# Linear attention: the inverses of the diagonal blocks are doubled from 16 to 64 rows in small array squares, and the solve substitutes between the two halves of 64 rows

## What is computed

```python
def _step(S, xs):
    qt, kt, vt, gt, bt = xs
    S = S * jnp.exp(gt)[..., None, None]
    pred = jnp.einsum('bhk,bhkv->bhv', kt, S)
    delta = (vt - pred) * bt[..., None]
    S = S + jnp.einsum('bhk,bhv->bhkv', kt, delta)
    return (S, jnp.einsum('bhk,bhkv->bhv', qt, S))
...
q = l2norm(q) * dk ** (-0.5)
k = l2norm(k)
...
o = o * jax.lax.rsqrt(jnp.mean(o * o, -1, keepdims=True) + EPS) * norm_weight
o = o * jax.nn.silu(gate)
return o.reshape(b, t, VALUE_DIM) @ Wo
```

## Time and profile before

| | us |
|---|---|
| median of 3 runs | 1380.96 |
| lowest, highest | 1378.22, 1382.22 |
| the profiled execution, its own time | 1384.09 |
| its span | 1382.5 |

### The profile page before, as it was taken

One profiled execution on the slowest core, in us unless ns is written; L12 is line 12 of the kernel. 1 busy time (PEld: TensorE's weight loads), 2 busy tenths in 40 slices (PEclk: granted clock), 3 DMA queues, 4 the chain that ended last, 5 costly groups with the idle time before them and its releaser, 6 DMA issues. The chain is left out here.

```text
span 1382.5 us, 24134 instructions
## 1 busy us (share of the span) xinstructions
PE 1207.8 (87%) x8826; PEld 1027.0 (74%) x8826; DVE 881.8 (64%) x2593; ACT 612.7 (44%) x1559; POOL 94.7 (7%) x103
## 2 busy tenths in 40 slices
PE   4999999899999974999899997279999999898478
PEld 3888789788878873888788897257777777677255
DVE  3767376375737656666567565688778887775423
ACT  3635454353444433434343432455675557444211
POOL 1000000000000001000000001110222022211000
PEclk9999999999999976999999996669999999999689
DMA  8010000000000020000000001100000000000322
GB/s 277 1 62 1 1 1 1 0 0 0 0 1 1 1 85 0 1 1 0 3 1 0 1 1 48 53 9 20 27 27 2 27 28 27 2 2 2 99 71 98
DMA packets 25722, 33.96 MB, mean 25 GB/s; under 512 B 4781, under 2 KB 21005, under 8 KB 25613
## 3 DMA queue, kind: packets, MB, share of 16 engines
q1 hardware_dynamic: 25612, 32.52, 7.2%
HBM read 30.34 MB, written 2.17 MB: 24 GB/s over the span
## 5 line engine op out<-in xcount | busy, mean ns | idle before, releaser
L986 PE MATMUL b_ps<-ln_high,b_high 128*128 128x512 f32 x256 | 102.2, 399 | 26.1 <-PEq L61 20.9
L333 DVE TENSOR_REDUCE a_negmax<-a_ps 128x1 f32<-128x128 f32 x128 | 37.2, 291 | 115.5 <-PE a_ps L514 106.9
L986 PE MATMUL b_ps<-ln_high,b_low 128*128 128x512 f32 x256 | 101.9, 398 | 0.0
L986 PE MATMUL b_ps<-ln_low,b_high 128*128 128x512 f32 x256 | 101.8, 398 | 0.0
L889 DVE TENSOR_TENSOR gate_up_raw<-gate_up_raw,b_ps 128x512 f32<-128x512 f32 x64 | 43.2, 686 | 91.7 <-PE b_ps L986 59.6
L553 PE MATMUL a_ps<-a_wo_high,a_oT 128*128 128x256 f32 x512 | 94.9, 284 | 2.0 <-DVE a_oT L359 2.0
L1013 PE MATMUL b_ps<-b_wd_high,b_mid 128*128 128x256 f32 x512 | 96.4, 283 | 0.0
L945 ACT ACTIVATE gate_up_raw<-b_ps 128x512 f32<-128x512 f32 x64 | 37.5, 598 | 121.0 <-PE b_ps L986 120.9
L477 PE MATMUL a_ps<-ln_high,a_w_high 128*128 128x512 f32 x160 | 69.1, 432 | 15.5 <-PEq L61 15.5
L553 PEld LDWEIGHTS a_ps<-a_wo_high,a_oT 128*128 128x128 f32 x512 | 79.7, 189 | 2.9 <-DVE a_oT L359 2.9
L1013 PEld LDWEIGHTS b_ps<-b_wd_high,b_mid 128*128 128x128 f32 x512 | 80.7, 189 | 0.6
(11 more groups left out here) (356 smaller groups left out, 3118.1 us busy)
## 6 DMA issues: line engine op xcount, KB each, us to landing
d_slots<-in_D_packed SPq DMA_DIRECT2D x16, 433.0 KB, 4.7
c_a_all<-a_scratch SPq DMA_DIRECT2D x8, 768.0 KB, 3.7
x<-in_hidden SPq DMA_DIRECT2D x4, 512.0 KB, 10.6
...
```

What stands on the lines that cost most here:

```text
L986: mm = nc.tensor.matmul(ps[:, bank, :], wpart, xpart, start=(j == 0), stop=(j == len(passes) - 1))
```

## The change

The block diagonal of 16x16 inverses isn't spread to 128x128 any more. VectorE's `seeds` writes the inverses into 32-wide rows (`inv16T`) and transposes them (`inv16`). TensorE then doubles them: `pair_part` and `pair_inverses` form the missing 16x16 corners of the 32x32 inverses, as products of 32x32x32 on single squares of the array (48 and 84 products for the 12 units); `quarter_part` and `quarter_inverses` form the corners of the upper and lower 64x64 inverses (24 and 36 such products). VectorE's `join_pairs` subtracts; ScalarE copies the results out and places them into `firstT` and `secondT` (`place_second`, `place_first`, `place_off`: nine instructions on 32 partitions). `half_part` forms, for each unit, the block under the diagonal times the lower inverse (12 products of 64x64x64). `solve` applies the two 64x64 inverses to the right side with a stationary operand of 128x64, `substitute` subtracts from the lower 64 rows what the solved upper rows give (12 products, 64x64 stationary). The four `step`s, N, its transpose and its square, `copy_n`, `copy_z` and POOL's `inverses` are gone. `copy_y` is done by row halves, four times.

The orders of TensorE, VectorE and ScalarE are changed too: `scores(m, 0)` goes ahead of jobs 0 and 1, `turn_values` goes up, jobs 4 and 5 go behind `outputs(s, 0)`, `project_out` and `all_norms` go down; on ScalarE `solved_keys` stays behind `silu(c, 2)`; on VectorE `keep_state`, `second_values` and `mean_square` go up among the columns, and `join_pairs` stands between `products` 3 and convolutions 3 to 5. PSUM banks are dealt anew, and `turn_out(d)` waits for the values of d+2. The core of the diff (indentation cut; first VectorE, then ScalarE, then TensorE):

```diff
+    def seeds(m):
+        nc.vector.tensor_tensor(
+            inv16T[:].rearrange("p u (b t) -> p u b t", b=2),
+            inv[:, :, 1:SUB + 1].rearrange("p u (o t) -> p u o t", o=1).to_broadcast([P, UNITS, 2, SUB]),
+            sides[:].rearrange("p (o b k) -> p o b k", o=1, k=1).to_broadcast([P, UNITS, 2, SUB]),
+            ALU.mult).then_inc(S["seed_ready"], 1)
+        dve.wait_ge(S["seed_ready"], at("seed_ready", m, 1))
+        nc.vector.transpose(flat(inv16[:]), flat(inv16T[:])).then_inc(S["seed_ready"], 1)
+
+    def join_pairs(b):
+
+        dve.wait_ge(S["a_done"], at("a_done", b, 1))
+        if b >= 1:
+            dve.wait_ge(S["half_copied"], at("half_copied", b - 1, 2))
+        nc.vector.tensor_tensor(flat(inv32T[:]), flat(inv16T[:]), ps[:, INV32_BANKS[0], 0:WIDE32],
+                                ALU.subtract).then_inc(S["pair_ready"], 1)
+        dve.wait_ge(S["a_done"], at("a_done", b, 2))
+        nc.vector.tensor_tensor(flat(inv32[0:96]), flat(inv16[0:96]), ps[0:96, INV32_BANKS[1], 0:WIDE32],
+                                ALU.subtract).then_inc(S["pair_ready"], 1)
...
         run(m, column_sum, 1)
         for h in range(DH):
             run(c, scan, h)
-        run(c, convolve, 6, 7)
-        run(m, columns, 2, 3)
-        run(c, convolve, 7, 8)
-        run(m, columns, 3, 4)
-        run(c, convolve, 8, 9)
-        run(s, step, 1, 0)
+        run(c, convolve, 6, 9)
+        run(m, columns, 2, 4)
+        run(s, keep_state)
+        run(m, off_diagonal, 0)
         run(m, columns, 4, 5)
-        run(s, step, 1, 1)
-        run(m, off_diagonal, 0)
-        run(m, columns, 5, 6)
         run(m, off_diagonal, 1)
-        run(m, columns, 6, 7)
-        run(s, step, 2, 0)
-        run(m, column_product, 7)
-        run(s, step, 2, 1)
+        run(m, columns, 5, 7)
         run(m, off_diagonal, 2)
-        run(m, column_sum, 7)
-        run(m, column_product, 8)
+        run(m, columns, 7, 8)
+        run(s, second_values)
         run(c, convolve, 9, 10)
-        run(m, column_sum, 8)
+        run(m, columns, 8, 9)
         run(c, convolve, 10, 11)
-        run(m, column_product, 9)
-        run(s, step, 3, 0)
-        run(m, column_sum, 9)
+        run(m, columns, 9, 10)
         run(c, convolve, 11, 12)
-        run(s, step, 3, 1)
+        run(s, mean_square, 0)
         run(m, column_product, 10)
         run(c, convolve, 12, 13)
         run(m, column_sum, 10)
-        run(s, keep_state)
+        run(c, convolve, 13, 14)
         run(m, column_product, 11)
-        run(c, convolve, 13, 14)
+        run(c, convolve, 14, 15)
         run(m, column_sum, 11)
-        run(c, convolve, 14, 15)
+        run(s, mean_square, 1)
         run(m, column_product, 12)
-        run(s, second_values)
+        run(c, convolve, 15, 16)
         run(m, column_sum, 12)
-        run(c, convolve, 15, 16)
+        run(d, add_out)
         run(m, column_product, 13)
-        run(s, mean_square, 0)
+        run(c, convolve, 16, 17)
         run(m, column_sum, 13)
-        run(c, convolve, 16, 17)
+        run(c, keys)
         run(m, column_product, 14)
-        run(d, add_out)
+        run(c, convolve, 17, 18)
         run(m, column_sum, 14)
-        run(c, keys)
-        run(m, column_product, 15)
-        run(c, convolve, 17, 18)
-        run(m, column_sum, 15)
-        run(s, mean_square, 1)
-        run(m, first_inverse)
+        run(m, columns, 15, 16)
+        run(m, seeds)
         if d == LAST:
...
                 channels.tap(act, c, j)
-        for q in range(PAIRS + 1):
-            run(s, copy_n, q)
+        run(s, copy_part16)
+        run(m, values_by_token, 0)
+        run(m, values_by_token, 1)
+        run(s, place_second)
+        run(s, copy_part32)
+        run(s, place_first)
         if d == LAST:
             n.copy(act, ps, 0)
         run(d, copy_oT, 0)
         if d == LAST:
             n.copy(act, ps, 1)
             n.copy(act, ps, 2)
-        run(s, copy_n, PAIRS + 1)
-        run(s, copy_n, PAIRS + 2)
+        run(s, place_off)
         run(m, fold_even)
         if inside(c):
             channels.silu(act, c, 0)
             channels.silu(act, c, 1)
-        for q in range(2 * PAIRS, 3 * PAIRS):
-            run(s, copy_n, q)
+            channels.tap(act, c, 2)
+            channels.tap(act, c, 3)
+        run(s, copy_part64)
         run(s, copy_y, 0)
         run(s, copy_y, 1)
-        if inside(c):
-            channels.tap(act, c, 2)
         run(m, second_keys)
-        run(s, copy_z, 0)
-        run(s, copy_z, 1)
-        run(m, values_by_token, 0)
-        run(m, values_by_token, 1)
-        if inside(c):
-            channels.tap(act, c, 3)
+        run(s, copy_y, 2)
+        run(s, copy_y, 3)
         if inside(c):
             channels.silu(act, c, 2)
+        run(s, solved_keys)
+        run(c, all_squares)
+        run(s, copy_wkT)
+        if inside(c):
             channels.tap(act, c, 4)
             channels.tap(act, c, 5)
-        run(c, all_squares)
-        run(s, solved_keys)
-        run(s, copy_wkT)
         run(s, squares, 0)
         run(s, save_output, 0)
...
+    def pair_part(b):
+
+        pe.wait_ge(S["seed_ready"], at("seed_ready", b, 1))
+        pe.wait_ge(S["l_ready"], at("l_ready", b, PAIRS))
+        if b + 1 < BATCH:
+            pe.wait_ge(S["conv_step"], at("conv_step", b + 1, CONVS))
+        for u in range(UNITS):
+            for q, rows in enumerate(QUARTERS):
+                mm = nc.tensor.matmul(ps[rows, PART16_BANK, cols32(u)], low[rows, b % 2, u, rows],
+                                      inv16T[rows, u, :], start=True, stop=True)
...
+    def half_part(b):
+
+        upper, lower = HALF_ROWS
+        if b == 0:
+            pe.wait_ge(S["cleared"], at("cleared", 0, 1))
+        pe.wait_ge(S["half_copied"], at("half_copied", b, 1))
+        for i, us in enumerate(UNIT_SETS):
+            for u in range(us.start, us.stop):
+                mm = nc.tensor.matmul(ps[upper, PART64_BANKS[i], cols64(u)], low[lower, b % 2, u, upper],
+                                      secondT[lower, u, :], start=True, stop=True)
...
+        src = right[:, b % 2, s]
+        for i, (h, half, cols) in enumerate(rights(s)):
+            for rows, inverse in zip(HALF_ROWS, (firstT, secondT)):
+                mm = nc.tensor.matmul(ps[rows, SET_BANKS[s], cols], inverse[:, h * HALVES + half, :],
+                                      src[:, cols], start=(i == 0), stop=False, skip_group_check=True)
...
+    def substitute(b, s):
+
+        upper, lower = HALF_ROWS
+        pe.wait_ge(S["pc_copied"], at("pc_copied", b, 2))
+        pe.wait_ge(S["y_copied"], at("y_copied", b, s + 1))
+        for h, half, cols in rights(s):
+            mm = nc.tensor.matmul(ps[lower, SET_BANKS[s], cols], part64[upper, h * HALVES + half, :],
+                                  y[upper, s, cols], start=False, stop=True, skip_group_check=True)
...
     for t in range(BATCH + 2):
         c, m, s, d = t + 1, t, t - 1, t - 2
+        run(m, scores, 0)
         run(c, job, 0)
         run(c, job, 1)
-        run(m, scores, 0)
-        run(s, n_product, 0)
-        run(s, n_product, 1)
-        run(s, n_product, 2)
+        run(s, pair_part)
         run(m, scores, 2)
-        run(s, n_product, 3)
+        run(m, turn_values, 0)
+        run(m, turn_values, 1)
+        run(s, pair_inverses)
         if d == LAST:
             pe.wait_ge(S["saved"], at("saved", LAST, 2))
             n.turn(pe, ps, r.ident, 0)
             n.turn(pe, ps, r.ident, 1)
+        run(s, quarter_part)
         run(d, turn_out, 0)
         run(d, turn_out, 1)
         if d == LAST:
             n.turn(pe, ps, r.ident, 2)
-        run(s, n_product, 4)
         run(m, scores, 4)
-        for q in range(PAIRS + 2, 3 * PAIRS):
-            run(s, n_product, q)
-        run(s, solve_blocks, 0)
-        run(s, solve_blocks, 1)
+        run(s, quarter_inverses)
+        run(s, half_part)
+        run(s, solve, 0)
+        run(s, solve, 1)
         run(c, job, 2)
         run(c, job, 3)
+        run(s, substitute, 0)
+        run(s, substitute, 1)
         run(m, turn_keys)
-        run(s, step, 0, 0)
-        run(s, step, 0, 1)
-        run(m, turn_values, 0)
-        run(m, turn_values, 1)
-        run(s, step, 1, 0)
-        run(s, step, 1, 1)
         run(m, turn_low, 0)
         run(m, turn_low, 1)
-        run(s, step, 2, 0)
-        run(s, step, 2, 1)
+        run(s, new_state)
         run(m, turn_low, 2)
-        run(c, job, 4)
-        run(s, step, 3, 0)
-        run(s, step, 3, 1)
-        run(c, job, 5)
-        run(s, new_state)
-        run(d, project_out, 0)
         run(s, turn_solved_keys)
         run(s, outputs, 0)
-        run(c, all_norms)
+        run(c, job, 4)
+        run(c, job, 5)
         run(s, known)
+        run(d, project_out, 0)
         run(d, project_out, 1)
         run(s, outputs, 1)
+        run(c, all_norms)
         run(m, gates, 0)
         run(m, gates, 1)
```

216 lines of the change are left out of this document (115 added, 101 removed).

## The result

The changed kernel takes 1484.25 us (median of 4 runs, 1481.02 to 1486.78), the kernel before 1381.47 in the same session: a ratio of 1.0748, 95% interval 1.072 to 1.0775. The forecast was 1480 with a range of 1425 to 1515. The profiled execution took 1486.78 us with a span of 1485.2.

A forecast was written before the change was run, and what follows sets the result against it. TensorE's work was taken to bound the attention pipeline; new waits in the queues (+63 us) and clock loss behind them (+36) gave +99 on 1384.1, 1483, stated as 1480 us, range 1425 to 1515.

The forecast's parts named there:

- if a square costs far from 0.030: Stated sign of being wrong: a 32x32x32 square record on TensorE costing far from 0.030 us.
- Bound and sign: Attention pipeline: TensorE's work falls only 1.1 us an iteration, its waits grow by 12.0, so the kernel gets slower.
- The waits: TensorE's waits in one period of the new order, walked: 15.3 us, against 3.3 in the old order.
- what is left on it, `queries`: POOL without `inverses`: the remaining `queries` waits for the same roots and ends before VectorE's `keys`; no cost.
- The chain: Late norms, then roots, `scan_starts`, output squares, `mean_square`, keys: TensorE waits 4.4 us ahead of `scores(m, 0)`.
- All_norms now comes after outputs(s, 1): Start of the path to the keys: only the gates (2.7 us) lie between the norms and the next scores.
- Squares, 0.030 us a record: TensorE's 384 square records an iteration, priced from the spacing in `outputs`: 11.5 us; bounds 0.015 and 0.060 a record.
- The floor of 0.025: About 60 cycles of overhead per matmul, 0.025 us a record at 2.4 GHz; would lower the forecast about 15 us.
- The clock: Each wait over 1.9 us brings 1.2 GHz, costing about 1.5 us; four waits in six iterations: +36 us.
- No clock loss: Rival: waits as walked, without half clock behind them: +63 us, 1444 us; chance 0.15.
- Cheap squares: Rival: square records below 0.030 us in good overlap, with clock loss: 1439 to 1465 us; chance 0.2.
- The other side: Rival: TensorE kept fed, only copy waits (3.85 us) remain, squares overlap fully at 0.015: 1335 us; chance 0.07.

The follow-up runs named there:

- four moves: Changed kernel with project_out, turn_keys and scores(m, 0) moved on TensorE and two convolution steps earlier on VectorE, no work changed: 1395.9 us, ratio 1.0112.
- the kernel before with two moves: Kernel before with all_norms(c) put behind outputs(s, 1) on TensorE and mean_square(s, 1) ahead of column_product 14 on VectorE: 1396.09 us, ratio 1.0111.
- the first search: Changed kernel's steps with the orders of TensorE, ScalarE and VectorE searched by a walk of the queues: 1376.41 us, ratio 0.999.
- the best run: Changed kernel's steps with orders searched further, the walk's clock falling after stretches with too much waiting: 1372.74 us, ratio 0.9928.

## Why the prediction was right, and where it was not

The time came out 4 us from the forecast, and the way it goes was right: slower, through TensorE's waits and its clock. The nearness is in part luck, since sizes were off with opposite signs, and one of its own signs of being wrong came true: "if a square costs far from 0.030". For the period from 1113.63 to 1175.16, 61.5 us, against the forecast's 56.2 and 6 of clock:

- **Bound and sign.** That the work of TensorE hardly decides and its waits do: shown. Reordering alone took back 88 us with four moves and 108 to 112 with all; taking out eleven twelfths of the squares took back 15.
- **The waits.** Forecast 15.3 us a period, measured 16.9: 0.97 at `place_off` (0.8), 2.20 before `substitute` (2.4), none of note at `new_state` (0.65), 2.44 before `turn_solved_keys` (3.85), 3.09 before `project_out` (3.2), 7.05 before the scores (4.4), and 1.16 of issue. The scores' wait is 2.6 larger. 2.5 of it are the two column products slowed beside POOL; the step that failed is "what is left on it, `queries`": `gated` on POOL, which in the kernel before runs at another time, was left out. That the gate's product on POOL is what slows them is read from when they run and end, not from a run without it. VectorE's waits at `mean_square` (9.42 for 6.6) and `keys_by_token` (3.69 for 3.1) and `fold_odd` (3.64 for 4.4) are where the walk put them.
- **The chain.** "All_norms now comes after outputs(s, 1)" was named as the start. Putting it back gave 14 us, putting the projection off 34, so the chain had two starts, and the second cost more. (The two were tried one by one from the changed kernel, not together.)
- **Squares, 0.030 us a record.** By the rows 0.010 on four quarters and 0.016 on two: 384 records take 4.8 us, not 11.5. This is the term that was most mis-sized, by 6.7 us a period. What the row of 64 columns had shown as spacing was not mostly issue. Some of it came back as stops, 1.2 us an iteration, which the prediction didn't know. Between two stops the price is 0.031, near the forecast's number for a reason that isn't in it.
- **The floor of 0.025.** The Trainium skill, page "TensorEngine Tiling (Array Packing)", section "Instruction Overhead", states about 60 cycles for each matmul, by the prediction's estimate 0.025 us a record. The records on four quarters don't keep to it: they start 0.010 us apart, and the measurement decides. The sum with 0.025, 1465, would have been 19 too low, since other terms were low.
- **The clock.** Forecast 6 us a period (four waits, 1.5 each). Without it the work would be 40.9 - 6.7 + 0.6 (`half_part` and `substitute` 3.5 for 2.9) = 34.8; the trace has 61.5 - 16.9 = 44.6, so 9.8 are left over, and the clock accounts for them: it is at half from 1113.6 to 1118.3, from 1138.8 to 1152.4 and from 1155.9 to 1162.7, 25.1 us with 3.4 of waiting in them, and if all of the other 21.7 us had taken twice its time, 10.9 would be lost. The step that failed is that a wait costs 1.5 and then is over. After the change, waits of 2.20 and 2.44 us stand 10 us apart and the clock is at half throughout from 1139 to 1152; the stretches join. The rule itself, a loss behind each wait of over 1.9 us, wasn't in the rows either: the forecast's own had one behind 1.35 and none behind 1.69, four waits of 2.2 in the kernel before with two moves had none, and two of 0.83 and 0.90 in the first search had 17 us of it.
- **Rivals.** No clock loss (1444): out, by a granted clock of 0.75. Cheap squares (1439 to 1465): the condition was right, 0.010, and the time wrong, since the freed time returned as waits and clock. The other side (1335): it asked for orders that keep TensorE fed; with such orders the best run gave 1372.7. Stops and half clock remain in it, and VectorE is busy for 36 us of a period that would have to be 39; which of these keeps it from 1335 was not shown.

So -6.7 (squares) + 0.6 (`half_part`, `substitute`) + 1.6 (waits) + 3.8 (clock, as what is left over) = -0.7 on 62.2 gives the measured 61.5. Three of the five steady periods are longer, up to 66.7, and their average is 63.7. That the total came to the forecast is luck in this sense: work that was 6 us a period too dear stood against waits and clock that were 5 too cheap. Of the other signs, VectorE's wait, TensorE's waits and its busy share (74% of the window) came as listed, and the periods, 59.4 to 66.7, ran over the listed 56 to 63.

What stays open: why the first two steady periods are 4 to 5 us longer than the third; what in waits, stops and squares lowers the clock; and whether the kernel before would gain from the same search of its orders, which was not tried.
